# Flamingo block with experts on one core: the shared experts' first hidden layer is computed earlier, and the first loads are cut into pieces

## The chip, the cores and the metric

The kernel runs on 1 core of one Trainium2 chip. The metric is the device time of one execution in microseconds (us). Before the change the median of 3 runs is 1692.69 us (1691.71 to 1694.25).

## The reference, cut to what matters

x has 16 sequences of 128 tokens with 512 features; the reference is four stages, each on a layer norm of x and added to x with a gate.

```python
x = x + tanh(g_xattn[0]) * retention(_layernorm(x), ctx)       # decay-masked linear attention, group norm, relu gate
x = x + tanh(g_ffn[0])   * experts(_layernorm(x))              # below
x = x + tanh(g_xattn[1]) * attention(_layernorm(x), ctx)       # fp8-rounded projections, two softmaxes
x = x + tanh(g_ffn[1])   * dense(_layernorm(x))

# experts: 8 routed experts, the best 2 for each token, and a shared one of twice the width
logits = xf @ gate_w;  top_logits, top_idx = top_k(logits, 2)
h = gelu(einsum('nd,edh->neh', xf, w1) + b1);  out_e = einsum('neh,ehd->ned', h, w2) + b2
routed = einsum('ne,ned->nd', gates, out_e)
shared = gelu(xf @ shared_w1 + shared_b1) @ shared_w2 + shared_b2
```

## The kernel before

The 2048 tokens are 16 tiles of 128 rows (B = 16), worked on in 4 chunks (C = 4) of 4 tiles (J = 4, CW = 512 tokens); features are 4 tiles of 128 (KT = 4). fp32 products are made as three fp32r products of high and low parts (`three_products`, L95 to L99). Each engine runs its own in-order program, written out by hand, and waits on semaphores; transfers are issued in order by SP (the sync engine's queue) and by POOL. Nothing reorders work within an engine. The stages in order, with the times of the profiled execution:

- `Retention` (L276 to L545), 0 to 96 us. SP loads the parameters, then the chunks of x, and weights. DVE makes each chunk's statistics (L457 to L461), ACT the root, DVE the normalised rows (L463). PE squares WhT (L395), transposes the rows (`turn`, L355 to L361), ACT and DVE split them into high parts (`high`, L419) and low parts (`low`, L474), and PE projects (`projected`, L364: one group of three products a head) and makes the gate (`gated`, L370: 48 products a chunk).
- `Values` (L547 to L779), 96 to 191 us: five roles for each chunk, `scored`, `headed`, `turned`, `projected`, in an order that `steps` (L572) gives to PE, ACT and DVE alike. `scored(c)` leaves bank 0 to 3 (ACT copies them to uT, L678), `headed(c)` banks 4 to 7 (ACT copies to o_sb, L685; DVE statistics, ACT root L687, DVE yn L731), `turned(c)` transposes yn (L641), ACT copies to yT (L694), DVE multiplies (z, L740), ACT and DVE split z (L700, L744), `projected(c)` makes the output rows. The next stage's gate weight is loaded here and its first chunks are normalised, transposed and split (`Sorting.turn`, `high`, `low`), into xT, 32 KB each for the high and the low parts of all tokens.
- `Sorting` (L844 to L1181), 191 to 223 us: logits, each token's best two experts (DVE), counts by three matmul groups (L1033 to L1035), a long DVE chain that places every token (L1123 to L1154), 32 matmuls that turn it into lists (L1039).
- `Routed` (L1287 to L1469), 223 to 396 us: 39 slots of 128 gathered rows through their expert. Beside it SP loads and stores the attention's prepared weights.
- `SharedAndQuantised` (L1471 to L1727), 396 to 502 us. For each chunk PE makes the shared layer's hidden rows (`hidden`, L1503: 4 blocks f of 12 products), ACT the Gelu twice (full and high part, L1567, L1568), DVE the low part (L1637), PE the output rows (`outputs`, L1518: for each tile a bias product L1529 and 12 products). DVE combines each row with its two gathered expert rows (`combine`, L1656), adds PE's rows (`added`, L1645), makes statistics (L1664, L1666) and normalises the chunk (L1675); PE transposes it (`turn`, L1549); ACT scales it for four weights (`scaled`, L1582), DVE rounds it to fp8 in three passes (`rounded`, L1684, L1686, L1690), SP stores it (L1726). `outputs` of tile n waits for the sum of tile n - 2; a rounding waits for the store two before it.
- The attention (from L2117 on), from 502 us, is 64 steps, and the dense layer closes. SP's program at its head (L2246 to L2262) is one order: stores 0 to 3, the first rows' load (L2235), weights KV and WQ (L2239), stores 4 to 7, weights WQX, the context's first piece (L2224), weights KVX, the next pieces, further stores. PE's first matmul there (L2356) waits for the last `added`.

SBUF is placed by hand (`mem.at(name, kb, ...)`), so tiles that share an address are kept apart by waits.

## Time and profile before

| | us |
|---|---|
| median of 3 runs | 1692.69 |
| the profiled execution | 1690.65 |
| its span | 1688.9 |
| PE busy | 1625.2 (96%) |
| ACT busy | 1104.6 (65%) |
| DVE busy | 1081.9 (64%) |
| POOL busy | 482.0 (29%) |

The profile is of one execution; its times are from the start of the span, which is 1.75 us shorter than the execution's time. A busy share says how much of the span an engine had an instruction in work; where PE was idle is read from the timeline, which names for each stretch of idle time the event that ended it. Four stretches hold PE's waits before 502 us: the begin, the values' stage around 120 us, the sorting, and the passage from the shared stage to the attention.

### The profile page before, as it was taken

What the parts mean: (1) busy time and instruction counts of PE and PEld (TensorE: products, weight loads), DVE (VectorE), ACT (ScalarE), POOL (GpSimd) and SP (SyncE); (2) the same over time, 40 slices, a digit from 0 to 9 for tenths busy, and PEclk for the clock granted to TensorE, in tenths of its full rate; (3) what the DMA queues carried; (4) which work ended last, traced back from release to release, by engine and by line L of the source; (5) the groups of instructions that cost most, each with busy time, mean ns of one, the idle gap of its engine ahead of it and who ended that gap; (6) DMA issues with size and microseconds to landing.
All of it is one profiled execution on the core that took longest, in us unless ns stands there. A gap on an engine that the chain in (4) does not pass through costs nothing.

```text
span 1688.9 us, 27156 instructions
## 1 busy us (share of the span) xinstructions
PE 1625.2 (96%) x9136; PEld 1337.6 (79%) x9136; DVE 1081.9 (64%) x2115; ACT 1104.6 (65%) x2981; POOL 482.0 (29%) x513
## 2 busy tenths in 40 slices
PE   6989869999999999999999999999999999999998
PEld 5888746666777888888788888788888788887887
DVE  6258854444886677777777776666666666788322
ACT  3454225553657988888888888887787887885100
POOL 1000122223424333342333433423423334331000
PEclk9999979999999999999999999999999999999999
DMA  6120648995673233364343353121152131110011
GB/s 244 50 81 26 225 177 278 324 312 186 213 257 135 64 146 117 130 267 152 118 151 132 113 221 141 40 104 56 39 197 115 39 112 56 38 45 1 25 38 38
DMA packets 74820, 219.67 MB, mean 130 GB/s; under 512 B 6288, under 2 KB 14480, under 8 KB 68304
## 3 DMA queue, kind: packets, MB, share of 16 engines
q1 hardware_dynamic: 69024, 199.56, 32.4%
q0 software_dynamic: 5680, 18.62, 3.6%
q8 instruction: 66, 1.08, 0.3%
q14 instruction: 50, 0.41, 0.1%
HBM read 157.60 MB, written 60.56 MB: 129 GB/s over the span
## 4 chain that ended last, share of the span: by engine, by line
PE 76%; ACT 4%; DVE 3%; DMA 3%; POOL 1%; issue 1%; ACTq 0%; POOLq 0%; DVEq 0%
PE bank L2356 10%; PE bank L2357 10%; PE bank L97 7%; PE bank L98 7%; PE bank L99 7%; PE bank L2417 7%; PE bank L2435 6%; PE bank L2448 6%; PE bank L2406 5%; PE bank L1347 3%; PE bank L1367 3%; PE bank L2427 3%; DMA s_rows<-x_rows,t_tok 2%; PE bank L1327 1%; ACT t_sc L2575 1%
## 5 line engine op out<-in xcount | busy, mean ns | idle before, releaser
L2686 DVE TENSOR_TENSOR t_hn<-bank,t_rs 128x256 f32<-128x256 f32 (+1 forms) x256 | 130.9, 553 | 139.3 <-POOL t_rs L2321 73.1
L2356 PE MATMUL bank<-t_slot,t_x_q 128*128 128x512 f32 x512 | 205.5, 401 | 0.0
L2318 POOL TENSOR_SCALAR t_ve<-t_ss 128x4 f32<-128x4 f32 (+1 forms) x128 | 25.9, 202 | 617.6 <-DVE t_ss L2682 608.4
L2357 PE MATMUL bank<-t_slot,t_x_q 128*128 128x512 f32 x512 | 200.3, 391 | 0.0
L2575 ACT ACTIVATE t_sc<-bank,t_mx 128x128 f32<-128x128 f32 x512 | 184.4, 456 | 3.5 <-DVE t_mx L2706 3.5
L2321 POOL TENSOR_TENSOR t_rs<-t_ve,t_mhalf 128x4 f32<-128x4 f32 (+1 forms) x128 | 171.0, 1336 | 10.6
L2575 ACT ACTIVATION_READ_ACCUMULATOR t_sc<-bank,t_mx 128x1 f32 x512 | 151.8, 296 | 0.0
L2613 ACT ACTIVATE t_y<-bank,smooth 128x128 bf16<-128x128 f32 x512 | 139.7, 402 | 1.9 <-PE bank L2435 1.9
L2417 PEld LDWEIGHTS bank<-t_hT 128*128 128x128 f32 x1024 | 120.2, 191 | 16.8 <-ACT t_hT L2602 16.2
L2417 PE MATMUL bank<-t_hT 128*128 128x128 f32 x1024 | 131.0, 281 | 2.3 <-ACT t_hT L2602 2.3
L2356 PE MATMUL bank<-t_slot,t_x_kv 128*128 128x256 f32 x512 | 125.3, 283 | 2.1 <-DVE x_res L1645 1.4
L2357 PE MATMUL bank<-t_slot,t_x_kv 128*128 128x256 f32 x512 | 125.6, 283 | 0.0
L2435 PE MATMUL bank<-t_pT,t_vv 128*128 128x256 f32 x512 | 121.1, 379 | 0.0
L2448 PE MATMUL bank<-t_wp,t_cq 128*128 128x512 f16 x512 | 121.0, 379 | 0.0
L2713 DVE RECIPROCAL t_ri<-t_sm 128x4 f32<-128x4 f32 x128 | 22.8, 178 | 149.4 <-ACT t_sc L2575 149.4
L2357 PEld LDWEIGHTS bank<-t_slot,t_x_q 128*128 128x128 f32 x512 | 96.3, 188 | 18.7
L2356 PEld LDWEIGHTS bank<-t_slot,t_x_q 128*128 128x128 f32 x512 | 96.4, 188 | 18.7
L2552 ACT ACTIVATE t_sqk<-bank 128x256 f32<-128x256 f32 x128 | 57.3, 456 | 77.3 <-PE bank L99 74.1
L2406 PEld LDWEIGHTS bank<-ident,t_hn 128*128 128x128 f32 x768 | 87.6, 141 | 22.7 <-DVE t_hn L2686 10.7
L2406 PE MATMUL bank<-ident,t_hn 128*128 128x128 f32 x768 | 97.3, 274 | 7.7 <-DVE t_hn L2686 7.7
L2356 PEld LDWEIGHTS bank<-t_slot,t_x_kv 128*128 128x128 f32 x512 | 97.7, 191 | 5.1 <-issue 2.7
L97 PE MATMUL bank<-t_slot,t_c_hi 128*128 128x512 f32 x256 | 100.4, 392 | 0.0
(324 smaller groups left out, 4161.7 us busy)
## 6 DMA issues: line engine op xcount, KB each, us to landing
t_xh<-xq_scratch SPq DMA_DIRECT2D x64, 512.0 KB, 3.8
t_slot<-w_ready SPq DMA_DIRECT2D x16, 2048.0 KB, 9.3
t_cr<-in_ctxT_dram SPq DMA_DIRECT2D x64, 256.0 KB, 2.7
y_rows<-s_y SPq DMA_DIRECT2D x39, 256.0 KB, 3.4
e_w<-in_w_units_dram SPq DMA_DIRECT2D x8, 1024.0 KB, 11.9
w_rows<-in_w_qkv_dram SPq DMA_DIRECT2D x8, 1024.0 KB, 7.1
w_ready<-w_hi SPq DMA_DIRECT2D x8, 1024.0 KB, 6.2
w_ready<-w_lo SPq DMA_DIRECT2D x8, 1024.0 KB, 8.2
```

Of the source, the lines that this page charges most:

```text
L97: nc.tensor.matmul(out, a_hi, b_hi, start=first, stop=False)
L98: nc.tensor.matmul(out, a_hi, b_lo, start=False, stop=False)
L2321: nc.gpsimd.tensor_tensor(rs[:, lo:hi], ve[:, lo:hi], mhalf[:, lo:hi], ALU.pow).then_inc(rs_in, 1)
L2356: nc.tensor.matmul(out, x_in[:, k, :], w[0][:, k, a:b], start=k == 0, stop=False)
L2357: last = nc.tensor.matmul(out, x_in[:, k, :], w[1][:, k, a:b], start=False, stop=k == KT - 1)
L2406: last = nc.tensor.transpose(b3[out][:, n, :], hn[:, h, :], env.ident[:])
L2417: last = nc.tensor.matmul(b3[4 + part][:, h, :], hT[:, (1 - part) * QH + h, :], hT[:, KH + (1 - part) * QG + h // 2, :], start=True, stop= ...
L2435: last = nc.tensor.matmul(bank[6 + part][:, g * 256:(g + 1) * 256], vv[par][:, (1 - part) * QG + g, :], pT[:, h:h + 2, :], start=True, sto ...
L2448: last = nc.tensor.matmul(bank[5][:], cq[par][:, h, :], wp[:, h, :], start=h == 0, stop=h == KH - 1)
L2575: last = nc.scalar.activation(sc[:, h, :], b3[4 + part][:, n, :], ACT.Exp, bias=mx[:, h:h + 1], accum_out=sm[:, h:h + 1])
L2613: nc.scalar.activation(y[:, part, ramp(h)], b3[6 + part][:, h, :], ACT.Copy, scale=env.smooth8[:, n:n + 1]).then_inc(y_in, 1)
L2686: nc.vector.tensor_tensor(hn[:, lo:hi, :], b3[bk][:, 0:hi - lo, :], rs[:, lo:hi].unsqueeze(2).broadcast_to([P, hi - lo, P]), ALU.mult).the ...
```

## The change

1. The begin. x's first chunk is loaded as four tiles with a semaphore each, ahead of the parameters; DVE makes each tile's statistics as it lands. PE transposes tile by tile (`first_turn`) and `projected` waits for one low part a head, not for four. DVE makes the first low parts before chunk 1's statistics.
2. `Values.steps`: chunk 1's `headed` goes ahead of chunk 0's `turned`.
3. The inner weights of the shared layer (two units of 512 KB) are also loaded behind the gate's weight, split by two ACT copies (`first_high`) and two POOL subtractions (`first_low`).
4. The hidden rows of the shared layer for chunk 0 are made in the sorting: blocks 0 and half of 1 ahead of the counts' matmuls, the rest behind them (`first_hidden`). Their Gelu passes go over the inputs of that chunk in xT (`first_gelu`), which nothing else needs any more; the low parts are made in routed steps 2, 3, 6 and 7. DVE waits for blocks 0 and 1 before it writes at_slot and for all four before it writes `same`, as those tiles share addresses with the new weights.
5. The shared stage begins with `hidden(1)`, then `outputs(0)` and `outputs(1)`; `turn(0)` follows. ACT's and DVE's orders are written out anew. SP waits for `outputs(0)` ahead of its first store.

```diff
 Retention.sync
+        for j in range(J):
+            sp.dma_start(env.x_res[:, j, :], dram["x"][j]).then_inc(self.tile_in[j], 16)
         sp.dma_start(env.par[:], dram["params"]).then_inc(self.par_in, 16)
-        rows(0)
 Retention.tensor
+        def first_turn():
+            for j in range(J):
+                pe.wait_ge(self.normed, j + 1)
+                for k in range(KT):
+                    last = nc.tensor.transpose(bank[k][:, ramp(j)], self.xn[0][:, j, ramp(k)], env.ident[:])
+                    if j == J - 1:
+                        last.then_inc(self.turned, 1)
         def projected(c):
-            pe.wait_ge(self.lo_in, c * KT + KT)
             for h in range(KT):
+                pe.wait_ge(self.lo_in, c * KT + h + 1)
...
-        turn(0)
+        first_turn()
 Retention.vector
+                for j in range(J):
+                    dve.wait_ge(self.tile_in[j], 16)
+                    v.bn_stats(env.st[:, j, :], env.x_res[:, j, :]).then_inc(self.stats, 1)
...
+        low(0)
         statistics(1)
-        low(0)
 Values.steps
                 attention[0](i)
+            if i == 1:
+                attention[1](i)
             if 1 <= i <= C:
                 turned(i - 1)
-            if i < C:
+            if i < C and i != 1:
                 attention[1](i)
 Values.gpsimd
+            if 1 <= c <= 2:
+                so.first_low(pool, c - 1)
 Values.scalar, projected
                 self.so.high(act, 0)
+                self.so.first_high(act, 0)
+                self.so.first_high(act, 1)
 Sorting.load_gate
+        for u in range(2):
+            sp.dma_start(self.units.first_raw[u][:].rearrange("p k n -> p (k n)"),
+                         self.env.dram["w_units"][E + u][:, 0:KT * HU]).then_inc(self.wg_in, 16)
 Sorting.tensor
         turn_logits(3)
+        sh.first_hidden(pe, 0, range(KT))
+        sh.first_hidden(pe, 1, range(2))
         pe.wait_ge(self.made, self.MADE)
...
                          ).then_inc(self.sort_ps, 1)
+        sh.first_hidden(pe, 1, range(2, KT))
+        sh.first_hidden(pe, 2, range(KT))
+        sh.first_hidden(pe, 3, range(KT))
         pe.wait_ge(self.at_in, 1)
 Sorting.scalar
+        for f in range(sh.FS):
+            sh.first_gelu(act, f)
         act.wait_ge(self.b2_raw_in, 32)
 Sorting.vector
+        dve.wait_ge(sh.h_ps, 2)
         v.tensor_tensor(self.at_slot[:], ...
...
+        dve.wait_ge(sh.h_ps, sh.FS)
         v.tensor_tensor(self.same[:], ...
 SharedAndQuantised
+    def first_gelu(self, act, f):
+        act.wait_ge(self.h_ps, self.FS)
+        nc.scalar.activation(self.h0[:, f, :], bank[:], ACT.Gelu, bias=bias)
+        nc.scalar.activation(self.h0_hi[:, f, :], bank[:], ACT.Gelu, bias=bias).then_inc(self.h_in, 1)
...
     def tensor(self, pe):
-        self.hidden(pe, 0, range(self.FS))
+        self.hidden(pe, 1, range(self.FS))
         self.outputs(pe, 0)
-        for c in range(1, C):
-            self.hidden(pe, c, range(self.FS))
-            self.turn(pe, c - 1)
-            self.outputs(pe, c)
+        self.outputs(pe, 1)
+        self.turn(pe, 0)
+        self.hidden(pe, 2, range(self.FS))
+        self.outputs(pe, 2, range(2))
+        self.turn(pe, 1)
+        self.outputs(pe, 2, range(2, J))
+        self.hidden(pe, 3, range(self.FS))
+        self.turn(pe, 2)
+        self.outputs(pe, 3)
...
     def vector(self, dve):
+        for f in range(self.FS):
+            self.low(dve, 1, f)
+        for j in range(J):
+            self.combine(dve, 0, j)
+            self.row(dve, 0, j)
+        for j in range(J):
+            self.combine(dve, 1, j)
+            self.row(dve, 1, j)
+            if j == 0:
+                self.normalise(dve, 0)
+        self.combine(dve, 2, 0)
+        self.rounded(dve, 0, 0)
...
+        self.row(dve, 2, 3)
+        self.combine(dve, 3, 0)
+        self.rounded(dve, 1, 1)
+        self.low(dve, 3, 0)
+        self.normalise(dve, 2)
+        self.combine(dve, 3, 1)
+        self.low(dve, 3, 1)
+        self.rounded(dve, 1, 2)
+        self.low(dve, 3, 2)
+        self.combine(dve, 3, 2)
+        self.low(dve, 3, 3)
+        self.rounded(dve, 1, 3)
+        self.combine(dve, 3, 3)
+        self.row(dve, 3, 0)
+        for j in range(1, 3):
+            self.row(dve, 3, j)
+            self.rounded(dve, 2, j - 1)
+        self.row(dve, 3, 3)
 attention, sync
         ready.all_stored(sp)
-        sp.wait_ge(sh.h_ps, 2 * sh.FS)
+        sp.wait_ge(sh.y_ps, J)
```

`row` is `added` and `statistics` of one tile. `first_hidden(pe, f, ks)` makes the products of block f for the given k, in banks 4, 5, 2 and 6.

## Rows read from the trace of the kernel before

**Rows 1.** Page, part 1: busy us (share of the span), instructions.

```profile
PE 1625.2 (96%) x9136; PEld 1337.6 (79%) x9136; DVE 1081.9 (64%) x2115; ACT 1104.6 (65%) x2981; POOL 482.0 (29%) x513
```

**Rows 2.** Timeline, the begin: start, us, engine, line, op, tiles, [idle before, releaser].

```profile
2.79 1.28 ACT L416 ACT_TABLE_LOAD   x1
...
6.75 2.47 DVE L89 BATCH_NORM_STATS2 st<-x_res 128x6 f32<-128x512 f32 x4 [6.75 <-DMA x_res<-in_x_dram]
...
7.45 2.07 PE L395 MATMUL bank<-a_whT 128*128 128x128 f32 x8 [7.45 <-DMA a_whT<-in_WhT_dram]
...
12.39 3.65 PE L361 MATMUL bank<-ident,a_xn 128*128 128x128 f32 x16 [2.87 <-DVE a_xn L471]
...
12.45 4.52 POOL L348 TENSOR_TENSOR a_wg_lo<-a_wT,a_wg_hi 128x2048 fp32r<-128x2048 f32 x1 [10.92 <-ACT a_wg_hi L431]
...
16.92 2.47 DVE L477 TENSOR_TENSOR a_xT_lo<-bank,a_xT_hi 128x512 fp32r<-128x512 f32 x4
...
19.53 0.77 PE L97 MATMUL bank<-a_xT_hi,a_m_hi 128*128 128x512 f32 x1 [3.49 <-DVE a_xT_lo L477]
...
24.68 0.39 PE L97 MATMUL bank<-a_xT_hi,a_wg_hi 128*128 128x512 f32 x1
```

**Rows 3.** Timeline, the values' stage, 109 to 129 us.

```profile
109.53 2.78 ACT L694 ACTIVATE v_yT<-bank,par 128x512 f32<-128x512 f32 x4
...
118.59 2.04 ACT L678 ACTIVATE v_uT<-bank 128x512 f32<-128x512 f32 x4
...
118.93 1.92 DVE L731 TENSOR_SCALAR v_yn<-v_o_sb,v_mv,v_rs 128x512 f32<-128x512 f32 x4
...
120.90 3.68 PE L641 MATMUL bank<-ident,v_yn 128*128 128x128 f32 x16 [2.83 <-DVE v_yn L731]
...
124.37 4.96 PE L632 MATMUL bank<-a_wh,v_uT 128*128 128x128 f32 x32
```

**Rows 4.** Windows: stretch, its length, busy us of each engine, PEclk, DMA share, GB/s.

```profile
120.00:122.00 2.00, 1.10 (x5) 1.10 (x6) 0.84 (x2) 0.63 (x2) 0.00 (x0) 0.52 0.91 346
```

**Rows 5.** Timeline, the sorting, 203 to 222 us.

```profile
203.47 1.91 PE L1019 MATMUL bank<-fold,r_lgT 128*128 128x8 f32 x16
...
209.48 0.77 PE L1033 MATMUL bank<-r_scan,r_tri 128*128 128x128 f32 x2 [4.10 <-DVE r_scan L1111]
...
214.04 1.46 DVE L1149 TENSOR_TENSOR r_at_slot<-r_cols,r_slot 128x1248 f16<-128x1248 f32 x1
...
221.51 1.25 PE L1039 MATMUL bank<-r_at_slot,r_at_row 128*128 128x39 f16 x32 [10.61 <-DVE r_at_row L1154]
```

**Rows 6.** Timeline, the shared stage, 407 to 502 us.

```profile
407.10 0.50 PE L1529 MATMUL bank<-r_b,r_gT 32*128 32x512 f32 x1
...
410.48 0.50 PE L1529 MATMUL bank<-r_b,r_gT 32*128 32x512 f32 x1
...
412.44 1.57 DVE L1656 SCALAR_TENSOR_TENSOR x_res<-z_back,t_gates,x_res 128x512 f32<-128x512 f32 x2
...
437.39 0.68 DVE L1684 TENSOR_SCALAR z_y<-z_y 128x2048 f16<-128x2048 bf16 x1
...
440.92 0.68 DVE L1684 TENSOR_SCALAR z_y<-z_y 128x2048 f16<-128x2048 bf16 x1
...
474.15 0.70 DVE L1690 TENSOR_SCALAR z_xs<-z_y 128x2048 int16<-128x2048 int16 x1 [2.18 <-DMA xq_scratch<-z_xs]
...
490.79 0.32 SPq L2239 DMA_DIRECT2D t_slot<-w_ready  x1
...
501.85 0.36 PE L2356 MATMUL bank<-t_slot,t_x_kv 128*128 128x256 f32 x1 [1.44 <-DVE x_res L1645]
```

**Rows 7.** Chain that ended last, 396 to 560 us: start, us, what.

```profile
396.25 0.25 PE bank L97
```

**Rows 8.** Tile t_slot (the weights' slots), 395 to 560 us: its DMAs.

```profile
DMA to landing us min/median/max: 7.8/8.4/14.5
```

**Rows 9.** Tile z_xs (the stored rows), 395 to 560 us: its DMAs.

```profile
DMA to landing us min/median/max: 2.9/3.3/8.4
```

More of the change, by code:

```diff
@@ L1516, in hidden, with outputs @@
             last.then_inc(self.h_ps, 1)
-    def outputs(self, pe, c):
+    def outputs(self, pe, c, js=range(J)):
         nc, env = self.nc, self.env
-        for j in range(J):
+        for j in js:
             n = c * J + j
@@ L1586, in scalar @@
     def scalar(self, act):
-        for c in range(C):
-            for f in range(self.FS):
-                self.gelu(act, c, f)
-            if 0 < c < C - 1:
-                for k in range(KT):
-                    self.scaled(act, c - 1, k)
+        for f in range(self.FS):
+            self.gelu(act, 1, f)
+        self.scaled(act, 0, 0)
+        self.gelu(act, 2, 0)
+        self.scaled(act, 0, 1)
+        self.gelu(act, 2, 1)
+        self.gelu(act, 2, 2)
+        self.gelu(act, 2, 3)
+        self.scaled(act, 0, 2)
+        self.scaled(act, 0, 3)
+        self.scaled(act, 1, 0)
+        self.scaled(act, 1, 1)
+        self.gelu(act, 3, 0)
+        self.scaled(act, 1, 2)
+        self.gelu(act, 3, 1)
+        self.scaled(act, 1, 3)
+        self.gelu(act, 3, 2)
+        self.gelu(act, 3, 3)
     def combined(self, c, j):
@@ L1692, in rounded, with row @@
                                 ).then_inc(self.q_in, 1)
+    def row(self, dve, c, j):
+        self.added(dve, c, j)
+        self.statistics(dve, c, j)
     def vector(self, dve):
-        for c in range(C):
-            self.low(dve, c, 0)
-            if c:
-                self.normalise(dve, c - 1)
-            for f in range(1, self.FS):
-                if c:
-                    self.combine(dve, c, f - 1)
-                self.low(dve, c, f)
-            if c:
-                self.combine(dve, c, J - 1)
-            for j in range(J):
-                if c == 0:
-                    self.combine(dve, 0, j)
-                self.added(dve, c, j)
-                if 0 < c < C - 1:
-                    self.rounded(dve, c - 1, j)
-                self.statistics(dve, c, j)
-                if c == C - 1 and 1 <= j <= 2:
-                    self.rounded(dve, C - 2, j - 1)
@@ L1714, in vector @@
-        self.rounded(dve, C - 2, 2)
+        for f in range(self.FS):
+            self.low(dve, 1, f)
[9 more added lines that the diff above has]
+        self.rounded(dve, 0, 0)
+        self.low(dve, 2, 0)
+        self.normalise(dve, 1)
+        self.combine(dve, 2, 1)
@@ new lines, in vector @@
+        self.low(dve, 2, 1)
+        self.rounded(dve, 0, 1)
+        self.low(dve, 2, 2)
+        self.combine(dve, 2, 2)
+        self.low(dve, 2, 3)
+        self.combine(dve, 2, 3)
+        self.row(dve, 2, 0)
+        self.rounded(dve, 0, 2)
+        self.row(dve, 2, 1)
+        self.rounded(dve, 0, 3)
+        self.row(dve, 2, 2)
+        self.rounded(dve, 1, 0)
+        self.row(dve, 2, 3)
[3 more added lines that the diff above has]
+        self.normalise(dve, 2)
@@ L2854, in _ @@
         def _(pe):
-            so.tensor(pe)
+            so.tensor(pe, sh)
             ro.tensor(pe)
```

100 lines of the change are left out of this document (71 added, 29 removed).

## The prediction, made before the result was known

> **What bounds the kernel now.** I read the page first, for the share of each engine: TensorE (PE) is busy for 96% of the span, VectorE (DVE) and ScalarE (ACT) for about 65% [rows 1]. So only two kinds of saving count: PE work that goes, and PE waits that go. The diff touches the program up to about 502 us, so next I read the timeline of four stretches of it, and in each ask what ended PE's idle time.
>
> The begin: PE waits 2.87 us for the normalised rows and 3.49 us for the low parts, and between 19.53 and 24.68 twelve 512-column matmuls need 5.15 us, 0.43 each [rows 2]. In the shared stage 48 such matmuls take 10.85 us, 0.226 each (block from 396.25 to 407.10) [rows 6, 7]. The begin runs at half clock (1.2 GHz), whatever its clock column says.
>
> The values' stage: PE waits 2.83 us for the normalised values [rows 3], and the clock then stands at 0.52 [rows 4]; 16 transposes take 3.68 us and 32 small matmuls 4.96, until 129.33 [rows 3].
>
> The sorting: PE has nothing for 4.10 and again for 10.61 us while DVE makes the order [rows 5].
>
> The shared stage: from 396.25 [rows 7] to the first matmul of the attention at 501.85 [rows 6] are 105.6 us. PE is nearly gapless, but its last wait, 1.44 us, is for the last row's sum on DVE, and DVE itself has stood 2.18 us for a store [rows 6]. Both engines are near the bound there.
>
> **Begin.** x's first chunk comes in four pieces, each with its own statistics; its load, and the 1.28 us table load behind the tanh, no longer have their old order [rows 2]. The parameters now land behind 1 MB of x, at about 6.6, so the table is in at about 8.3 and the root follows. That costs nothing as long as it beats PE's own first task, the eight matmuls that end at 7.45 + 2.07 = 9.52 [rows 2]: the first tile is normalised by about 9.3. So the transposes start at 9.6 instead of 12.39, and end at 9.6 + 3.65 = 13.3. The four banks fill only with the last tile, so the copies of the high parts start at 12.8, and the low parts, 0.62 each [rows 2], end at about 14.1, 14.7, 15.4, 16.0, as the next statistics now stand behind them. Each head waits only for its own low part: the projection starts at 14.1 instead of 19.53. It takes 5.15 us at half clock, or 2.7 at the pitch of 0.226. The gate's matmuls so start between 19.25 and 16.97 (its low weights are done on POOL at 12.45 + 4.52 [rows 2]) instead of at 24.68: 5.4 to 7.7 us. PE now works from 7.5 with one short gap, so I take a clock that rises inside the projection: **7.0 us less**, bounds 4 and 8. What is late next is the second chunk's root, which ACT now does ahead of the projection's copies, at about 19.2; PE needs none of these copies before its transposes at about 28, so it is hidden behind the 10.9 us of gate matmuls.
>
> One rule speaks against the four pieces. In the trace a 256 KB load that stood right behind the 1 MB of x landed 0.70 us after it (7.45 against 6.75 [rows 2]): a small load in a full queue costs its share of bandwidth. The Trainium skill, "DMA: Bandwidth & Descriptors", section "Measured (HBM→SBUF, 128 partitions, SWDGE, issued from GpSimd)", says to batch loads to a MiB or more. If each piece paid for itself, the last would land late and the begin would give less: a rival below.
>
> **Values.** Chunk 1's `headed` goes ahead of chunk 0's `turned` on all three engines. PE no longer waits with nothing to do at 118: by my walk in the old trace's times it does `headed(1)` to 113.4 and the transposes to 115.2. But ACT now makes chunk 0's yT copies (2.78 us) only after chunk 1's root, at 115.7; PE's `scored(2)` needs their banks and starts at 116.7. Then DVE normalises (1.92) before it multiplies, ACT rounds the products, and only at 121.3 comes to the uT copies (2.04) [rows 3], which it now starts after the products where it started them at 118.59. PE transposes from 122.0, and `projected(0)` waits for an o_sb copy behind all this: 128.9, where it was 129.33 [rows 3]. So the wait of 2.83 us and the slow clock give way to three gaps of 1.4 to 1.7 us: **0.3 us less**. Bounds: 2 less if ACT catches up, 3 more if these gaps also halve the clock: 3.68 us for 16 transposes is 1.84 above the full pitch, and the first part of the 4.96 as well [rows 3].
>
> The three weight passes that go with it (two ACT copies of 128x1024, two POOL subtractions at half of 4.52 us [rows 2], two 512 KB loads on SP) fall between 118 and 183, where ACT and POOL wait for PE and the queue is empty: nothing. If a POOL pass blocked DVE it would cost at most its 2.26 us.
>
> **Sorting.** 18 matmuls (4.07 us) go into the wait of 4.10 and 30 (6.8 us) into the wait of 10.61 [rows 5]. DVE's new wait for two blocks stands before the pass at 214.04 [rows 5]; the blocks are done at 210.9 + 1.4 = 212.3. Behind it queue all passes that place the tokens, so late blocks would be paid in full. The counts' matmuls, six with the two that took 0.77 us at 209.48 [rows 5], now follow full work and no idle time, so I expect the full clock: **0.4 us less**; bounds 1 less and 2.2 more (30 at 0.43 are 12.8 us, against 10.61). The eight Gelu passes, 4.1 us at the pace of ACT's copies (2.04 for four [rows 3]), run behind the blocks, from 217.3, and end before the placing matmuls of 221.51 [rows 5] have led to any row; four subtractions of 0.62 us go between the routed steps, where DVE follows PE: nothing, at most 2.5 us if all four were exposed.
>
> **Shared stage.** PE loses one block, 10.85 us [rows 6, 7]. But DVE loses only four subtractions. Its way from the second row's combine (412.44, 16.2 us into the stage, unchanged since outputs still follow a hidden block) to the last sum: 15 combines of 1.57, 15 rows of 1.46 (the 3.53 us from 437.39 to 440.92 less a rounding), 10 roundings of 3 x 0.69 [rows 6], 8 subtractions of 0.62 [rows 2], 3 normalisations of 1.92 [rows 3]: 77.0, less 0.8 behind the sum, ends at 92.4. In the two output blocks that now follow each other it keeps PE's pace (3.38 us a row, from 407.10 to 410.48 [rows 6], instead of 3.03, for 7 rows): + 2.4. And the roundings wait for stores. The order on SP is four stores, the first rows' load, two weight loads of 2 MB, then store 4. The four roundings come later, so by my walk the weights go out at about 67 and store 4 right behind them. Weight loads landed after 7.8 to 14.5 us [rows 8], a store after up to 8.4 [rows 9]; so the store lands between 76 and 82.7, and DVE wants it at 78.2: 0 to 4.5 us. I take 1.9, in the middle, since two loads stand ahead of it and nothing else does. Sum 16.2 + 76.2 + 2.4 + 1.9 = 96.7 against 105.6: **8.9 us less**, bounds 4 and 10.85. PE alone would be there at 105.6 - 10.85 - 1.44 = 93.3, so DVE has the end.
>
> **Attention's start.** The last of four weight loads went out at 490.79, 11 us before 501.85 [rows 6], and the third well before it. Now both stand behind store 7, which comes with a late rounding, and go out together, 10.6 and 9.4 us before the attention. The second lands 8.4 to 14.5 us after it goes out [rows 8]; the context's first piece between them delays POOL's split and with it SP's next loads and store 8, for which DVE waits in front of the last normalisation. **1.7 us more**, bounds 0 and 3.5.
>
> **Sum.** -7.0 - 0.3 - 0.4 - 8.9 + 1.7 = -14.9. The profiled execution took 1690.65 (span 1688.9 and 1.75 around it): 1675.8. It lies 2.0 below the median of the runs, 1692.69, for which I give **1677.8**.
>
> **Rivals.** (A) All is hidden: begin 8, values 2, sorting 1, shared 10.85, start 0: 21.9 less, 1670.8. For it: PE's share. Against: DVE's sum above. Chance 0.09. (B) The three gaps in the values' stage halve the clock: 3.3 us dearer, 1681.1. Against it: the 2.83 us gap that did so [rows 3, 4] was longer than each. The Trainium skill, "TensorE: Matmul & The Clock Gate", section "A second HAM failure mode: psum-queue depth-cycling", says for it that short, frequent idle stretches between groups make the clock oscillate. Chance 0.14. (C) The loads and stores collide as badly as the worst rows: 2.6 more on DVE, 1.8 more at the start: 1682.2. Chance 0.13. (D) The small loads of x pay each for itself and the begin gives 3: 1681.8. Chance 0.03. (E) The moved layer does not do what it says: at half clock it outlasts its cover by 2.2 us and delays the sorting: 1680.4. Chance 0.03. (F) Slower: DVE's chain in the shared stage is stretched by its stores. If all twelve roundings stood as long as this one did, 2.18 us [rows 6], that is 26.2 instead of what I have, 1.9, and the kernel takes 1702; it turns slower from 17 us in all, 1.4 a rounding. Against it: only the fourth and fifth store meet the weights. Chance 0.03.
>
> **How the numbers follow.** Forecast 0.55, its own range 1674 to 1681. The range from 1671.5 to 1685 takes in B to E and half of A; it leaves out F, the rest of A and the joint tails of B and C, about 0.15. Within 0.2% (3.4 us, what a measurement of this kernel can tell from no change) needs B, C and D together: 0.03. Faster 0.94, slower 0.03.
>
> **What would show it.** The first transposes at 9.6 and the first gate matmul near 17.5; `projected(0)` in the values' stage about 7.5 us earlier than 129.33 with a clock at 1.00; no PE wait over 5 us in the sorting; the attention's first matmul about 16.6 us earlier than 501.85; one rounding that waits about 2 us for a store. Wrong would be: a last wait in the shared stage that PE's own work ends, or a clock of 0.5 where I have none.

## The result

The changed kernel takes 1689.88 us (median of 20 runs) where the kernel before, in the same runs, takes 1692.64: the ratio is 0.9981, 95% interval 0.9972 to 0.9989. That is 3 us less where 15 were forecast (1677.8, range 1671.5 to 1685.0). One of the 20 runs took 4245.87 us, and the ratio leaves it out. The profiled execution of the changed kernel took 1687.33, its span is 1685.6.

The two profiles side by side, stage by stage. Each stretch runs from the first matmul of one stage to the first of the next, read from the timeline of PE:

| stretch | before | changed | difference | forecast |
|---|---|---|---|---|
| start to the gate's first matmul | 24.68 | 17.68 | -7.00 | -7.0 |
| to `projected(0)` of the values | 104.40 | 103.75 | -0.65 | -0.3 |
| to the barrier behind the values | 64.33 | 64.32 | 0 | 0 |
| to the counts' matmuls | 16.07 | 18.75 | +2.68 | (in the next row) |
| to the placing matmuls | 12.03 | 11.41 | -0.62 | -0.4 |
| to the first expert matmul | 7.98 | 7.81 | -0.17 | |
| routed stage | 166.51 | 169.18 | +2.67 | 0 |
| shared stage | 105.85 | 104.75 | -1.10 | -8.9 |
| attention and dense, to the end | 1187.05 | 1187.95 | +0.90 | +1.7 |
| span | 1688.9 | 1685.6 | -3.3 | -14.9 |

So the begin gave what was forecast, and three stretches did not: the barrier, the routed stage and, above all, the shared stage.

The page of the changed kernel, part 1 (busy us, share of the span, instructions), answers to [rows 1]:

```profile
PE 1629.2 (97%) x9136; PEld 1336.7 (79%) x9136; DVE 1083.3 (64%) x2115; ACT 1105.9 (66%) x2983; POOL 487.2 (29%) x515
```

PE is busy for 4.0 us more than in [rows 1] with the same 9136 instructions. A busy time that grows while the work stays is the first sign of a slower clock under that work. The mean granted clock of the span doesn't show it (0.992, and 0.990 before), because PE has little to do in some of the slow stretches and much in others.

The begin, timeline (start, us, engine, line, op, tiles, [idle before, releaser]), answers to [rows 2]:

```profile
3.52 1.34 DVE L471 BATCH_NORM_STATS2 st<-x_res 128x6 f32<-128x512 f32 x2 [3.52 <-DMA x_res<-in_x_dram]
...
9.14 3.65 PE L361 MATMUL bank<-ident,a_xn 128*128 128x128 f32 x16
...
14.30 0.47 PE L97 MATMUL bank<-a_xT_hi,a_m_hi 128*128 128x512 f32 x1 [1.51 <-DVE a_xT_lo L491]
...
17.68 0.50 PE L97 MATMUL bank<-a_xT_hi,a_wg_hi 128*128 128x512 f32 x1 [0.41 <-POOL a_wg_lo L350]
```

The transposes follow PE's first task without a gap. The projection starts at 14.30 and its twelve products take 3.0 us (5.15 before), so most of it runs at full pitch. Only POOL's low parts hold the gate, for 0.41 us.

The values' stage and the stretch behind the barrier, windows (stretch, its length, busy us of each engine, PEclk, DMA share, GB/s), the first answers to [rows 4]:

```profile
120.00:122.00 2.00, 0.90 (x6) 0.65 (x6) 2.00 (x5) 2.00 (x5) 0.00 (x0) 1.00 0.88 352
...
188.00:192.00 4.00, 3.68 (x18) 3.48 (x18) 1.53 (x15) 1.20 (x2) 0.41 (x12) 0.50 1.02 263
```

PEclk, the last but two, is the granted clock of TensorE as a share of 2.4 GHz. It stood at 1.00 in the reordered values, where it had been 0.52, but at 0.50 behind the barrier, where the kernel before had 1.00. The barrier is PE's wait of 1.84 us in front of the second group of logits; it is the same in all profiles.

The sorting, timeline of PE, answers to [rows 5]:

```profile
190.25 3.65 PE L995 MATMUL bank<-ident,r_xn 128*128 128x128 f32 x16
...
215.91 1.25 PE L1080 MATMUL bank<-r_at_slot,r_at_row 128*128 128x39 f16 x32 [3.69 <-DVE r_at_row L1198]
```

The moved layer does what it says: the wait of 4.10 us for `r_scan` is gone, that of 10.61 is 3.69, and the first two of the counts' matmuls, at 204.50, take 0.45 us instead of 0.77, so they are at full clock. The half clock (1.2 GHz) stands ahead of it, in the logits: 16 transposes take 3.65 us, where experiment 2 shows 1.95 for them.

The shared stage, timeline, answers to [rows 6]:

```profile
412.41 0.75 DVE L1743 SCALAR_TENSOR_TENSOR x_res<-bank,gate_tanh,x_res 128x512 f32<-128x512 f32 x1 [1.47 <-remote]
...
461.23 0.91 SPq L2367 DMA_DIRECT2D t_slot<-w_ready  x2
462.35 5.55 SPq L1854 DMA_DIRECT2D xq_scratch<-z_xs  x2
...
477.28 0.69 DVE L1788 TENSOR_SCALAR z_xs<-z_y 128x2048 int16<-128x2048 int16 x1 [3.90 <-DMA xq_scratch<-z_xs]
...
478.63 0.50 PE L97 MATMUL bank<-z_w_hi,e_h_hi 128*128 128x512 f32 x1 [2.00 <-DVE e_h_lo L1735]
...
480.75 0.79 PE L97 MATMUL bank<-z_w_hi,e_h_hi 128*128 128x512 f32 x1 [1.16 <-DVE e_h_lo L1735]
...
488.22 0.75 DVE L1743 SCALAR_TENSOR_TENSOR x_res<-bank,gate_tanh,x_res 128x512 f32<-128x512 f32 x1 [2.34 <-PE bank L99]
...
494.68 1.58 POOL L2466 TENSOR_TENSOR t_c_lo<-t_cr,t_c_hi 128x512 fp32r<-128x512 f32 x1
495.17 1.68 DVE L1788 TENSOR_SCALAR z_xs<-z_y 128x2048 int16<-128x2048 int16 x1
...
497.65 0.36 PE L2484 MATMUL bank<-t_slot,t_x_kv 128*128 128x256 f32 x1 [2.72 <-DVE x_res L1743]
```

Tile `z_xs`, 391 to 530 us, its DMAs (answers to [rows 9]), and the window behind PE's two waits:

```profile
DMA to landing us min/median/max: 2.9/4.7/14.8
```

```profile
480.00:488.00 8.00, 7.25 (x16) 4.83 (x16) 5.64 (x10) 3.64 (x6) 0.00 (x0) 0.57 0.63 207
```

The lines from 461.23 to 488.22 are one chain, and it is to be read in order. Two weight loads of 2 MB go out at 461.23. Store 4 goes out behind them, at 462.35, and lands after 14.8 us. DVE stands 3.90 us for it. The low parts that DVE owes PE come late, so PE stands 2.00 and 1.16 us. Behind these the clock is 0.57 for 8 us and matmuls take 0.63 to 0.79 us. Now DVE waits for PE, 2.34 us. At the end POOL's split of the context falls together with a rounding, which takes 1.68 us instead of 0.69. The first line is a wait by itself: DVE's combine ended at 410.94 and PE's products for that row at 410.84, and the sum still starts at 412.41. The trace names no engine for it here.

The start of the attention, timeline of PE of the changed kernel and then of the kernel before, the first matmul behind the 16 that start at 497.65 and at 501.85 [rows 6]:

```profile
501.01 0.52 PE L97 MATMUL bank<-t_slot,t_c_hi 128*128 128x512 f32 x1
```

```profile
503.83 0.40 PE L97 MATMUL bank<-t_slot,t_c_hi 128*128 128x512 f32 x1
```

The same 16 matmuls take 3.36 us instead of 1.98. The granted clock of the first 4 us is 0.57, where the kernel before has 1.00.

### The profile page after: what moved, and what is told of

It reads as the page before. It is cut to its first block, busy times and chain, and to the rows that moved or that the text cites. A ratio compares the mean times of both kernels' runs of the same rounds, so it can differ in the third digit from the quotient of the medians.

```text
span 1685.6 us, 27163 instructions
## 1 busy us (share of the span) xinstructions
PE 1629.2 (97%) x9136; PEld 1336.7 (79%) x9136; DVE 1083.3 (64%) x2115; ACT 1105.9 (66%) x2983; POOL 487.2 (29%) x515
## 4 chain that ended last, share of the span: by engine, by line
PE 74%; DMA 5%; ACT 4%; DVE 4%; issue 1%; POOL 1%; ACTq 0%; POOLq 0%; DVEq 0%
PE bank L2484 10%; PE bank L2485 10%; PE bank L97 7%; PE bank L98 7%; PE bank L99 7%; PE bank L2545 7%; PE bank L2563 6%; PE bank L2576 6%; PE bank L2534 5%; DMA s_rows<-x_rows,t_tok 4%; PE bank L2555 3%; PE bank L1396 2%; PE bank L1416 2%; PE bank L1376 1%; DMA xq_scratch<-z_xs 1%
## 5 line engine op out<-in xcount | busy, mean ns | idle before, releaser
L2484 PEld LDWEIGHTS bank<-t_slot,t_x_kv 128*128 128x128 f32 x512 | 98.7, 193 | 5.5 <-issue 3.1
L2485 PEld LDWEIGHTS bank<-t_slot,t_x_kv 128*128 128x128 f32 x512 | 99.0, 193 | 2.4
```

The lines of the kernel that those rows point to most:

```text
L2484: nc.tensor.matmul(out, x_in[:, k, :], w[0][:, k, a:b], start=k == 0, stop=False)
L2485: last = nc.tensor.matmul(out, x_in[:, k, :], w[1][:, k, a:b], start=False, stop=k == KT - 1)
```

## The experiments

The times below are medians, the ratio is that to the kernel before in the same runs. "Stage" times are from each run's profile, as in the table above. The rows of all of them are gathered in one table at the end of this section. The expectations call the experiments by labels: 1 to 6 are e1 to e6, 7 is e7, and 8 to 11 are e9_short_rounding, e10_queue, e11_row_first and e12_load_later.

**1. The changed kernel once more.** Nothing edited.

> The changed kernel once more, nothing edited, for a second profile. In its first profile three places took more than forecast: the clock fell to half behind the barrier between the values' stage and the sorting (187.2 to 193.4 us, 2.7 us lost), PE waited 4.8 us in eight places for gathered rows between 229 and 391 us (2.7 us in three places in the kernel before), and the shared stage took 104.7 us. If these belong to the program (theory), all three come back within 0.5 us. If each execution draws them anew (rival), at least one of the first two differs by more than 1 us, and the shared stage still takes 103 to 106. The time is 1690 in either case.

1690.03 us, ratio 0.9970 (0.9954 to 0.9986). The barrier came back slow (18.69 us), the gathers cost 5.0 us, the shared stage 104.58 with the same chain: the store wait 3.80, PE's waits 1.87 and 1.15, half clock at 482 to 490, the last wait 3.08. The theory stands for these three places as far as two profiles go, and the shared stage's chain came back whole. The barrier's cost does not belong to the program, as experiment 2 shows.

**2. Store 4 ahead of the weights.**

```diff
         x_rows(0)
+        sh.store(sp, KT)
         weights(0, KV, kv_w)
         weights(0, WQ_, q_w)
-        for k in range(KT):
+        for k in range(1, KT):
             sh.store(sp, KT + k)
```

> One line moved on SP: the store of the second chunk's first quarter goes out ahead of the first two weight loads of 2 MB instead of behind them. In the changed kernel it landed after 14.8 us, DVE stood 3.90 us for it, PE then stood 2.00 and 1.16 us for low parts and ran at half clock for 6 us (3 us lost). Theory: that stall is where the shared stage's gain went. The store then lands in 3 to 5 us, DVE does not wait for it, PE has neither the two waits nor the slow clock, and from the first hidden matmul to the attention's first one are 97 to 99 us instead of 104.7: 6 to 8 us less than the changed kernel, about 1683. Rival: DVE's own work has the end, the waits only move, and 0 to 2 us are won: 1688 to 1690. If the weights, 1.5 us later, become late, the attention's start shows a wait for them.

1688.35 us, ratio 0.9971 (0.9959 to 0.9983): 1.7 less than the changed kernel by the medians, nothing by the ratios, and not 6 to 8. Inside the stage the theory holds: the 3.90 us store wait, the 2.00 and 1.16 us waits and the slow clock behind them are gone, and the stage takes 100.50 instead of 104.75. But it did not reach 97 to 99, and the attention took 1191.62 instead of 1187.95. Two lines say why. Window in the middle of the stage, and timeline of DVE behind the stage:

```profile
450.00:458.00 8.00, 8.00 (x27) 5.76 (x26) 5.46 (x10) 2.28 (x4) 3.98 (x4) 0.58 0.73 208
```

```profile
503.54 0.90 DVE L1788 TENSOR_SCALAR z_xs<-z_y 128x2048 int16<-128x2048 int16 x1 [6.47 <-DMA xq_scratch<-z_xs]
```

The clock fell behind two shorter waits for low parts, 0.35 and 1.16 us at 449.6, which the changed kernel has too (0.33 and 1.15 at 449.1) but where it kept its clock. And store 8 goes out at 497.42, behind the context's first piece and POOL's split of it, so that DVE stands 6.47 us in front of the last normalisation. The stall had been hiding a second one. This program, the same up to there, also passed the barrier at full clock (16.09 us), so what that place costs differs from one execution to the next. Timeline of PE behind the barrier, to be set against the line of 190.25 above:

```profile
188.80 1.95 PE L995 MATMUL bank<-ident,r_xn 128*128 128x128 f32 x16
```

**3. and 4. The parts apart.** Experiment 3 is the changed kernel with the begin of the kernel before, experiment 4 the kernel before with the new begin (item 1 of the change) alone.

> The changed kernel with the begin of the kernel before: x's first chunk in one load, chunk-wise transposes, one wait for all low parts. Everything behind the begin comes 7.0 us later. Theory: a gain at the begin goes through to the end, so this takes 7 us more than the changed kernel, 1697. Rival: where the barrier and the gathers fall in time decides what they cost, and the old begin puts them back: the clock stays at full behind the barrier and the gathers wait 2.7 us instead of 4.8, so only 2 to 4 us are lost: 1692 to 1694.

> The kernel before with the new begin alone. Theory: 7.0 us less than the kernel before, 1685.6, since all that follows is the same program. Rival: the earlier phase costs 2.7 us at the barrier and 2.1 us in the gathers, as in the changed kernel's profile, and only 2 to 4.5 us are won: 1688 to 1690.5.

Begin alone: 1687.54 us, ratio 0.9970 (0.9958 to 0.9981), 5.2 us less; the interval takes in 7.0. All but the begin: 1695.10, ratio 1.0010 (0.9998 to 1.0021), 2.3 us more, or nothing. The old begin costs the changed kernel 5.1 us. So the begin's gain goes through nearly whole, and the rest of the change is worth nothing by itself. Both times lie between what the theory and the rival had set. In experiment 3 the rival had the barrier right (16.08) and the gathers wrong (5.7 us).

**5. SP's order.** On top of 2:

```diff
         weights(0, KV, kv_w)
         weights(0, WQ_, q_w)
-        for k in range(1, KT):
-            sh.store(sp, KT + k)
+        sh.store(sp, KT + 1)
         sp.wait_ge(sh.h_ps, C * sh.FS)
         weights(0, WQX, qx_w)
+        sh.store(sp, KT + 2)
         context(0)
+        sh.store(sp, KT + 3)
         sp.wait_ge(sh.comb, 4 * C * 2)
         weights(0, KVX, kvx_w)
```

> As e2_store_first, and SP's queue reordered further: the third weight load of 2 MB goes out when the last hidden block is done, ahead of the stores that used to stand before it, and the context's first piece ahead of the last two stores and of the fourth weight load. In e2_store_first DVE then stood 6.47 us for the first store of the third chunk, which SP could not issue before 497.4 because it waits for POOL's split of that piece, and PE needed 1191.6 us from the attention's first matmul to the end instead of 1187 to 1189. Theory: the whole of it is SP's order. The piece lands 6 us earlier, that store goes out at about 492 (in the times of e2_store_first), DVE waits under 2 us for it, the attention takes 1187 to 1188, and the kernel takes 1683 to 1686. Rival: the queue is bound by its bytes, so another store lands late in place of this one, a DVE wait of 3 us or more shows elsewhere, and the time stays at 1687 to 1689.

1684.23 us, ratio 0.9951 (0.9933 to 0.9968). The shared stage takes 99.88, the attention 1187.68, as expected; DVE still stands 1.59 us for one store and 2.95 for store 8. With another order of issues on one queue the change gives 8.7 us instead of 3.

**6. Low parts first.** On top of 5, in DVE's order: `low(2, 2)` ahead of `rounded(0, 1)`, `low(2, 3)` ahead of `combine(2, 2)`, `low(3, 3)` ahead of `combine(3, 2)`.

> As e5_sp_order, and on DVE each of the last two low parts of the third and fourth hidden block goes ahead of the combine or rounding that stood before it. In all runs so far PE waits 0.35 and 1.16 us for low parts at the start of the third chunk's outputs, and in two of four profiles the clock fell to half for 8 us right behind them (3.4 us of full-speed work lost). Theory: these short waits are what brings the slow clock in the middle of the shared stage; without them PE waits there only 0.8 us, the clock stays at full from 440 to 485, and from the first hidden matmul to the attention's first are 96 to 98 us: 1 to 3 us less than e5_sp_order, about 1682. Rival: DVE has the end, so PE's waits only move behind the last row, and the time is that of e5_sp_order within 1 us.

1682.95 us, ratio 0.9936 (0.9919 to 0.9952), which can't be told from experiment 5. The stage takes 100.36 instead of 99.88. PE's waits for low parts are gone, but PE now stands 2.66 us for the fourth chunk's first row, and the clock falls behind that one, from 484 to 491. The rival had it right: DVE has the end, and PE's waits move.

**7. The reorder of the values alone, and the kernel before again.** Experiment 7 is the kernel before with item 2 of the change; 7b has nothing edited.

> The kernel before with one part of the change alone: in the values' stage the second chunk's heads go ahead of the first chunk's transposes. Theory: 2.83 us of waiting and the clock at half behind it are given up for four gaps of 1.1 to 1.5 us; from the gate's first matmul to the first projection 103.7 us instead of 104.4, so 0.3 to 0.9 us less in the whole, which this measurement can't tell from no change. Rival: the gaps halve the clock, and that stretch takes 105 to 107. The routed stage, the same program as before, shows once more what its gathers cost: 2.7 us of PE's waits if that belongs to the program, 4.5 to 6 if the kernel before drew a lucky execution.

> The kernel before once more, for a second profile of it. Theory: what the gathers cost is drawn by each execution. PE's waits for gathered rows in the routed stage, 2.7 us in its first profile and 4.8 to 6.2 in five others (one of them with this very routed and shared program), come to 4 to 6 us, and the stage takes 168 to 170 us instead of 166.5. Rival: the routed stage of the kernel before is the faster one, and it takes 166.5 again, within 0.5. The shared stage, which has no draw in it, takes 105.9 within 0.4.

Experiment 7: 1693.64 us, ratio 1.0008 (0.9996 to 1.0021): no gain. From the gate to `projected(0)` it takes 103.69. The kernel before needs 104.40 in its first profile, where the clock fell behind the wait of 2.83 us, and 102.42 in its second, where it did not (1.00 from 23.4 to 204). Against an execution that keeps its clock the reorder is 1.3 us dearer, against one that loses it 0.7 cheaper. And the routed stage, the same program in both, took 166.51 in the first profile and 171.70 in the second. Waits of PE in the routed stage (229 to 396 us) of the kernel before, second profile; in the first one the same line reads 3.2 us in 4 waits:

```profile
PE bank L1327 <- DMA s_rows<-x_rows,t_tok: 6.3, 7, 1.9
```

The kernel before had been profiled in the cheapest of its four routed stages. The shared stage came back at 106.02.

**8. A shorter rounding.** On top of 6, the first of each rounding's three passes is made for 8 of 2048 columns.

> As e6_sp_and_lows, and the first of the three passes of each of the twelve roundings (0.68 us, conversion and limits) is made for 8 of its 2048 columns, so the rounded rows are not those of the reference from there on. Ten of these passes stand in the shared stage, about 6 us of DVE's work there. Theory: DVE has the end of the shared stage. Then 4 to 6 us go, until PE's own work (93 us with the waits for the first rows) has it: hidden to attention 94 to 96.5 instead of 100.4, the kernel 1677 to 1679. Rival: the stores have the end (DVE stood 2.25 us for one), so a faster DVE only stands longer for them: 98 to 100, the kernel 1681 to 1683.

1680.15 us, ratio 0.9932 (0.9914 to 0.9949). The stage takes 95.68 instead of 100.36, inside the 94 to 96.5 of the theory; PE's last wait is 2.21, so DVE has the end of the shared stage, as the prediction said. Not all of the 4.68 us is the rounding's: experiment 6 had a wait of 1.45 us in front of the second row's sum and 1.72 for PE at half clock, and this one has neither. The whole came out above the 1677 to 1679 expected, with a routed stage of 173.46 in its profile, and its ratio can't be told from that of experiment 6.

**9. The queue once more.** On top of 6, the store `KT + 1` goes out between the first two weight loads, and the store `2 * KT` ahead of `context(1)`.

> As e6_sp_and_lows, and on SP the store of the second chunk's second quarter goes out between the first two weight loads instead of behind them, and the third chunk's first store ahead of the context's second piece. In e6_sp_and_lows DVE stood 2.25 us for the former and 4.29 us for the latter. Theory: both waits go (under 0.5 us each), hidden to attention takes 98 to 99.5 instead of 100.4, the attention 1187 instead of 1187.9, so 1.5 to 3 us less: 1680 to 1681.5. Rival: the second weight load, some 6 us later, is late for the attention and its matmuls wait for t_slot, or the store behind it lands late again: 1682 to 1684.

1682.00 us, ratio 0.9937 (0.9921 to 0.9954). DVE stands 1.23 us for one store and for store 8 not at all. The stage takes 97.31. Timeline of its last wait:

```profile
491.88 0.36 PE L2487 MATMUL bank<-t_slot,t_x_kv 128*128 128x256 f32 x1 [4.28 <-DVE x_res L1743]
```

PE had been done 4.28 us earlier, so its own work ends at 93.0 and DVE's at 97.3. The prediction had 93.3 and 96.7. The attention took 1187.72 and the weights were in time. The ratio is that of experiment 6, with a routed stage of 172.78.

**10. A row first.** On top of 9, `row(3, 0)` goes ahead of `rounded(1, 3)` and `combine(3, 3)`.

> As e10_queue, and on DVE the sum of the fourth chunk's first row goes ahead of a rounding and a combine. In e6_sp_and_lows PE stood 2.66 us for that sum (1.31 in e5_sp_order), and in e6_sp_and_lows its clock fell to half behind it, so that DVE then waited 1.72 us for PE. Theory: PE waits under 1 us there, no slow clock between 480 and 492, and hidden to attention takes 97 to 98.5: 1 to 2 us less than e10_queue, 1679 to 1680.5. Rival: DVE's work is the same and has the end, so the time is that of e10_queue within 0.7 us.

1681.53 us, ratio 0.9929 (0.9911 to 0.9948). PE waits for no row but the last, for 4.78 us, and the stage takes 97.31 again. The rival was right: DVE stood 0.62 us for a store and 0.53 for PE, and the rest is its own work.

**11. One load later.** On top of 10, in `Routed.sync`:

```diff
         ready.load(sp, 0)
-        ready.load(sp, 1)
         for s in range(SLOTS_N):
+            if s == 2:
+                ready.load(sp, 1)
             sp.wait_ge(self.y_in, s + 1)
```

> As e11_row_first, and the second of the two loads of 1 MB that SP issues together at the start of the routed stage goes out after the second slot's rows are stored, some 11 us later. In all twelve profiles so far PE waits 1.7 to 3.3 us for gathered rows some 12 us into the stage, right behind these two loads. Theory: a gather shares the DMA engines with whatever is in flight, and that is why the routed stage takes 166.5 to 173.5 us in executions of one and the same program. The first long wait then falls under 1 us, the stage takes 168.5 to 172 instead of 169.2 to 173.5 and the kernel 0.5 to 2 us less than e11_row_first: 1679.5 to 1681. Rival: the wait comes from the gathers' own speed (two were issued 2.4 us apart), and stays; or it only moves to the gather behind the later load: 1681 to 1682.

1678.66 us, ratio 0.9919 (0.9897 to 0.9941). The first wait for gathered rows, timeline of PE of experiment 10 and then of 11:

```profile
234.52 1.12 PE L1376 MATMUL bank<-ident,s_rows 128*128 128x128 f32 x4 [3.25 <-DMA s_rows<-x_rows,t_tok]
```

```profile
231.74 0.66 PE L1376 MATMUL bank<-ident,s_rows 128*128 128x128 f32 x4 [0.85 <-DMA s_rows<-x_rows,t_tok]
```

All waits for gathered rows sum to 3.5 us (6.7 in experiment 10). The mean granted clock over the first 25 us of the stage is 0.92 (0.82 in experiment 10, where it fell behind the wait of 3.25). The routed stage takes 168.59, less than in any of the nine profiles of the changed kernel and its versions, though only 0.6 less than the lowest of them. The first wait had been 1.7 to 3.3 us in all thirteen other profiles, so that the load made this gather late is shown. It didn't move either: behind the later load the waits stay at 0.5 us or less until 139 us into the stage. That it is worth the whole 2.9 us between the medians of 10 and 11 is not: by the ratios it is 1.7, and the intervals overlap. The shared stage, the same program as in experiment 10, takes 99.12 instead of 97.31: the wait in front of the second row's sum is there again (1.49 us), and DVE's store wait is 0.92 instead of 0.62. This is the fastest version: by the ratio 13.7 us (0.8%) below the kernel before.

| us | gate | to `projected(0)` | barrier to counts | routed | shared | to the end |
|---|---|---|---|---|---|---|
| before | 24.68 | 104.40 | 16.07 | 166.51 | 105.85 | 1187.05 |
| before again | 23.96 | 102.42 | 16.08 | 171.70 | 106.02 | 1186.84 |
| 4 begin only | 17.90 | 103.52 | 16.70 | 168.84 | 106.16 | 1186.87 |
| 7 values only | 24.54 | 103.69 | 16.07 | 170.76 | 106.13 | 1186.75 |
| 3 old begin | 24.83 | 103.69 | 16.08 | 169.51 | 106.89 | 1187.53 |
| changed | 17.68 | 103.75 | 18.75 | 169.18 | 104.75 | 1187.95 |
| 1 changed again | 19.09 | 103.77 | 18.69 | 170.19 | 104.58 | 1188.92 |
| 2 store first | 17.11 | 103.68 | 16.09 | 172.98 | 100.50 | 1191.62 |
| 5 SP's order | 17.54 | 103.63 | 16.07 | 170.49 | 99.88 | 1187.68 |
| 6 low parts first | 17.79 | 103.94 | 18.45 | 170.60 | 100.36 | 1187.91 |
| 8 short rounding | 17.57 | 103.71 | 16.09 | 173.46 | 95.68 | 1185.90 |
| 9 queue | 18.69 | 103.76 | 16.09 | 172.78 | 97.31 | 1187.72 |
| 10 row first | 17.68 | 103.55 | 16.72 | 173.48 | 97.31 | 1188.55 |
| 11 load later | 16.61 | 103.64 | 16.09 | 168.59 | 99.12 | 1188.65 |

## Why the prediction was wrong

The step that failed is the term of the shared stage: 8.9 us less were forecast, 1.10 less were measured. It priced DVE's wait for a store as that wait alone (1.9 us), and gave no price to what a late DVE does to PE. The term of 0 for the routed stage and the missing term for the barrier come next.

**Begin: right.** 7.00 us in the profiles, and by the means of ten profiles with the new begin (17.8) and four with the old (24.5) 6.7. The transposes came at 9.14 (9.6), the projection at 14.30 (14.1), the gate at 17.68 (17.5). The four small loads of x did not pay each for itself: two tiles' statistics stand from 3.52 to 4.86 and the other two end at 6.99, where the kernel before could only start at 6.75 [rows 2]. The rule behind rival D (the Trainium skill, "DMA: Bandwidth & Descriptors", section "Measured (HBM→SBUF, 128 partitions, SWDGE, issued from GpSimd)") did not decide here. In experiments 1 and 9 the gate came at 19.09 and 18.69, because the clock, full from about 11, was at half once more from 14.5 to 17.9.

**Values: right within its bounds, wrong in its reason.** The gaps are there (1.28, 1.24 and 1.10 us) and the clock stayed full. But the half clock that I counted as a cost of the old order is one that the old order pays only in some executions. By the means of three profiles with the old order (103.4) and eleven with the new (103.7) the reorder costs 0.3 us; experiment 7 sees no gain.

**Sorting: the sum was right, the barrier was left out.** The placing came 0.62 us earlier and all cover held. What I had not looked at is the barrier in front of it, where PE stands idle in every execution. In four of ten profiles of the changed kernel and its versions, the clock fell behind it, and that costs 2.4 to 2.7 us in three of them and 0.6 in one; of the four with the old sorting one lost 0.6. The ten are the same program from the gate up to there, with the same wait of 1.84 us, and had both, so the change doesn't settle it alone. Whether it makes it more frequent stays open: 2.4 us or more were lost in three of ten profiles with the new sorting and in none of four with the old.

**Routed stage: the step that took one execution for the program.** I set 0 and made the sum against a stage of 166.51. The same program then took 168.84, 170.76 and 171.70. The means are 169.5 for these four and 171.4 for the nine with the change. In every profile the stage is its own work, plus PE's waits for gathered rows (2.7 to 7.6 us), plus what the half clock costs in it, which is half of the time at half clock (0.5 to 4.4 us). Taking these two away leaves 162.2 to 163.9 us in all fourteen profiles, with means of 162.7 for the old routed stage and 163.1 for the nine. So of the 2.0 us between the means about 0.4 are the changed program's work, 0.8 are longer waits and 0.8 the clock. Whether the change makes the waits and the slow clock more frequent (the first loads go out 3.0 us into the stage instead of 4.1) is not settled: profiles measured together show 168.8 against 169.5 to 173.0 in one set, and 170.8 and 171.7 against 170.5 and 170.6 in another.

**Shared stage: the mechanism right, the price wrong, and the chain behind it missed.** This is the step that decided. DVE as the new bound, at 96.7 with a store wait, is what experiments 9 and 10 show (97.31, with store waits of 1.23 and 0.62). The changed kernel took 104.75, and the 8.05 between are: 0.3 until the second row's combine, 16.46 us into the stage, because the 396.25 of [rows 7] is not the stage's first matmul, which starts at 396.00 (the block is 11.1 us and the old stage 105.85); 1.1 in DVE's work, 79.7 us without its waits instead of 76.2 + 2.4, about as much as the collision with POOL takes (passes of 0.97 and 1.68 instead of 0.69); 2.0 for the store, 3.90 instead of 1.9, since it landed after 14.8 us, where the longest in [rows 9] was 8.4; 2.34 for PE at half clock; 0.72 for another of PE's rows; 1.47 for the wait in front of the second row's sum, which no term had; 0.15 to PE's first matmul. The 2.4 that I had set for PE's pace turned out to be DVE's own (3.29 us a row). The cause of the wait of 1.47 stays open: the traces name PE for it in some profiles and nobody in others, and in the changed kernel PE's products had ended before it. It is 1.4 to 1.5 us in ten of the fourteen profiles, three with the old shared stage among them, and absent in four. The old stage hides it (105.85 without, 106.0 to 106.2 with it). Where DVE has the end it counts in full: experiments 9 and 10 take 97.31 without it, 11 takes 99.12 with it.

The rest is one chain. A stall of DVE was priced as itself. It really passed to PE (3.16 us of waits), there to the clock, and back to DVE. Bounds of 0 to 4.5 for the store held; that no bound was set for what a late DVE does to PE was the error. Rival F had the right kind, a DVE chain stretched by its stores, but one store was enough for most of the loss, not all twelve.

**Attention's start: the number right, the mechanism not; luck.** 0.9 us more in the profile and 1.25 by the means of three and four, of 1.7 forecast. I had put it on the weight loads and on the context's first piece. But the last two weight loads go out 14.5 and 12.9 us ahead, and PE waits for neither. DVE does stand 2.68 us for store 8, at 502.43, but it stood 2.47 in the kernel before, and in experiment 9 that wait is gone and the attention still takes 1187.72. What the traces show is the clock: DVE has the end now, PE's last wait is 2.72 us instead of 1.44, and behind it the first 16 matmuls take 3.36 us instead of 1.98. They take 1.98 or 1.99 in the four profiles with the old shared stage and 2.5 to 4.3 in eight of the ten with the new one. In the other two, experiments 6 and 8, they take 1.98 and 1.99, behind waits of 0.94 and 2.21.

Together, by the means of the profiles: begin -6.7, values +0.3, barrier +0.7, placing -0.6, routed +2.0 (unsettled), shared -0.6, end +1.3: 3.6 us less, where the runs say 2.8 to 3.2. Of the eleven to twelve missing, eight are the shared stage. With SP's queue and DVE's low parts in another order 6.7 to 8.5 of the forecast 8.9 are there (99.12 in experiment 11, 97.31 in 9 and 10, against 105.85).

**The range** left out the case that came. A change of under 3.4 us was given 0.03 and was to need B, C and D together, and it came without B and D. The store wait stayed inside its bound of 4.5, but it brought the half clock with it, in a place where no rival had it. That is one of the signs that I had named as wrong: a clock of 0.5 where I have none. It stood there three times, behind the barrier, in the shared stage and at the attention's start.

## What to carry to other kernels

When an engine that had slack becomes the bound, look at each transfer for which it waits and at what is queued ahead of that transfer. A 512 KB store behind 4 MB of loads was a stall here, and the order of issues on one queue was worth more than the work moved. Price a new stall not by itself but with what it does to the engine that it feeds, the clock included. When the sum comes out right, check its terms too: here the attention's start had the right number for a wrong reason. Before a sum is made against one profile, take a second one of the same kernel: a stage of which nothing was changed differed by 5 us.

## What the runs showed of the hardware

**The same waits, another clock.** The same instructions, with the same idle time at the barrier (1.84 us), went on at full clock in some executions and at 0.57 to 0.58 over 8 us in others (2.4 to 2.7 us lost). The same holds for the waits of 0.35 and 1.16 us in the shared stage: the clock fell in experiments 2 and 3, not in the changed kernel's two profiles nor in experiment 5. The Trainium skill, "TensorE: Matmul & The Clock Gate", section "A second HAM failure mode: psum-queue depth-cycling", says of another kernel that short and frequent idle times between groups of matmuls let the clock swing. By that account these waits are the kind to fear, and the traces agree, but they also show that the same waits cost nothing in the next execution, and the values' stage with its three gaps kept full clock in all eleven profiles with the new order.

**A DVE pass beside a POOL pass.** In the shared stage's rows a rounding pass of 0.69 us took 1.68, from 495.17, while POOL's subtraction ran from 494.68 to 496.26: it ended 0.6 us after POOL. In the kernel before the same pass took 1.83 beside POOL's of 1.29. The Trainium skill, "SBUF — State Buffer", section "SBUF: two separate sides", says that some DVE modes and POOL share a pair of ports and whoever comes first holds it for its whole instruction; the traces agree, the DVE pass does its own 0.6 us after POOL has ended. Where the split fell earlier (experiment 5, 486.78) another pass took 1.80 instead of 0.66. Not every pair shows it: in the changed kernel the pass at 493.47 kept its 0.66 us, though the trace has POOL's copy from 492.72 to 494.59.

**What a transfer waits for.** Half of the 512 KB stores landed after 2.9 to 4.7 us, the one behind two loads of 2 MB after 14.8; in experiment 2, where it goes out ahead of them, DVE does not wait for it. PE waited 1.7 to 3.3 us for rows gathered by POOL behind two loads of 1 MB on SP's queue (thirteen profiles) and 0.85 behind one (one profile).
